# Causal mask of two grouped attentions: a DVE addition in the scores bank instead of two bf16 products per round

## The reference, cut to what matters

```python
# _L0_attn_b_ref: 32 query heads of 128, 8 key heads, rotary and compressed parts
scores = jnp.einsum('bhqd,bhkd->bhqk', q, k) * scale
causal = jnp.tril(jnp.ones((q_len, q_len), bool))
scores = jnp.where(causal[None, None], scores, jnp.asarray(-1000000000.0, dt))
attn = jax.nn.softmax(scores, axis=-1)
out = jnp.einsum('bhqk,bhkd->bhqd', attn, v)

# _L1_attn_a_ref: 32 heads, latent keys and values
scores = (jnp.einsum('bshd,bthd->bhst', q_nope, k_nope) + jnp.einsum('bshd,btd->bhst', q_pe, k_pe)) * scale
scores = jnp.where(causal[None, None], scores, jnp.finfo(scores.dtype).min)
probs = jax.nn.softmax(scores, axis=-1)
out = jnp.einsum('bhst,bthd->bshd', probs, v).reshape(b, s, NH * V_DIM)
```

## Time and profile before

| what | value |
|---|---|
| median of 3 runs | 2360.93 us |
| lowest and highest | 2348.55, 2364.01 us |
| the profiled execution: its own time | 2363.39 us |
| its span, first to last instruction | 2361.7 us |
| mean granted TensorE clock | 0.959 |
| attn0b's rounds, attn1a's rounds | about 540 to 1275 us, 1392 to 1887 us of the span |

### The profile page before, as it was taken

The page is one execution under the profiler, slowest core; times in us unless marked ns, Lnnn a source line. Parts: engine busy times, 40 slices in busy tenths (PEclk is TensorE's granted clock), DMA queues, the critical chain, the costliest instruction groups (busy, mean ns, idle before and its releaser), DMA issues. The chain is left out here.

```text
span 2361.7 us, 33423 instructions
## 1 busy us (share of the span) xinstructions
PE 2153.1 (91%) x11504; PEld 1480.1 (63%) x11504; DVE 1414.9 (60%) x2599; ACT 1093.5 (46%) x2639; POOL 840.2 (36%) x1062
## 2 busy tenths in 40 slices
PE   6999998887999999999997869999999986899988
PEld 4344366665777777777775656777777664554457
DVE  5777575416566556565663645666666555757756
ACT  4666653214444444444443535555555533325553
POOL 2000000534444444443442025555544412346621
PEclk9899999997999999999999979999999997989999
DMA  2000023651111111111110244433333201543310
GB/s 89 1 1 1 1 76 111 139 118 52 41 54 32 41 54 32 41 32 32 36 50 31 67 103 108 108 91 100 92 98 78 78 23 53 160 95 68 71 34 36
DMA packets 112542, 149.18 MB, mean 63 GB/s; under 512 B 39588, under 2 KB 52516, under 8 KB 110200
## 3 DMA queue, kind: packets, MB, share of 16 engines
q1 hardware_dynamic: 64376, 108.77, 16.3%
q0 software_dynamic: 48000, 38.28, 7.1%
HBM read 86.07 MB, written 27.26 MB: 48 GB/s over the span
## 5 line engine op out<-in xcount | busy, mean ns | idle before, releaser
L1842 POOL TENSOR_TENSOR attn0b_probs<-attn0b_probs,attn0b_recip 128x128 f32<-128x128 f32 (+3 forms) x256 | 192.5, 772 | 223.4 <-DVE attn0b_recip L2081 223.2
L2473 POOL TENSOR_TENSOR attn1a_probs<-attn1a_probs,attn1a_recip 128x128 f32<-128x128 f32 (+3 forms) x256 | 179.2, 721 | 232.9 <-DVE attn1a_recip L2656 232.3
L2529 ACT ACTIVATE attn1a_probs<-attn1a_scores,attn1a_negmax 128x128 f32<-128x128 f32 (+3 forms) x256 | 132.8, 524 | 174.5 <-DVE attn1a_negmax L2642 173.3
L1948 ACT ACTIVATE attn0b_probs<-attn0b_scores,attn0b_negmax 128x128 f32<-128x128 f32 (+3 forms) x256 | 132.8, 524 | 149.5 <-DVE attn0b_negmax L2074 148.3
L1956 ACT ACTIVATE attn0b_probsT<-attn0b_turned 128x128 f32<-128x128 f32 (+3 forms) x128 | 56.0, 438 | 245.7 <-PE attn0b_turned L2222 245.3
L2235 PE MATMUL attn0b_out<-attn0b_probsT,attn0b_v_now 128*128 128x512 f32 x320 | 155.6, 617 | 11.8 <-DVE attn0b_probsT L2088 11.8
L1468 DVE TENSOR_REDUCE attn0a_negmax<-attn0a_by_query 128x2 f32<-128x1024 f32 x128 | 152.3, 1219 | 21.3 <-PE attn0a_by_query L1555 21.3
L2642 DVE TENSOR_REDUCE attn1a_negmax<-attn1a_scores 128x2 f32<-128x256 f32 (+3 forms) x128 | 105.5, 824 | 70.6 <-PE attn1a_scores L2831 70.6
L2074 DVE TENSOR_REDUCE attn0b_negmax<-attn0b_scores 128x2 f32<-128x256 f32 (+3 forms) x128 | 104.8, 819 | 46.5 <-PE attn0b_scores L2211 46.5
L37 PE MATMUL attn0b_aux<-attn0b_wo_hi,attn0b_oT_hi 128*128 128x512 f32 x256 | 126.4, 494 | 1.4 <-DVE attn0b_oT_lo L2092 1.4
L2843 PE MATMUL attn1a_turned<-ident_f,attn1a_probs 128*128 128x128 f32 x640 | 115.8, 279 | 8.6 <-DVE attn1a_probsT L2650 7.2
(11 more groups left out here) (510 smaller groups left out, 6115.0 us busy)
## 6 DMA issues: line engine op xcount, KB each, us to landing
pre<-in_b_o SPq DMA_DIRECT2D x16, 1024.0 KB, 5.3
attn1a_qT<-attn1a_stage SPq DMA_DIRECT2D x128, 128.0 KB, 2.4
attn1a_qT<-attn1a_stage SPq DMA_DIRECT2D x64, 256.0 KB, 3.8
pre<-in_b_q SPq DMA_DIRECT2D x8, 1024.0 KB, 6.4
pre<-in_b_kv SPq DMA_DIRECT2D x5, 1024.0 KB, 5.8
attn0b_vals<-attn0b_v_out SPq DMA_DIRECT2D x16, 256.0 KB, 4.0
attn0b_keys_hi<-attn0b_part_hi POOLq DMA_DIRECT2D x32, 128.0 KB, 5.1
attn0b_keys_lo<-attn0b_part_lo POOLq DMA_DIRECT2D x32, 128.0 KB, 7.7
```

The lines of the kernel that those rows point to most:

```text
L1842: pool.tensor_tensor(x, x, recip[:, r % 2, e:e + 1].broadcast_to([P, (qt + 1) * P]), ALU.mult).then_inc(s_scaled, 1)
L1948: act.activation(probs[:, r % 2, e, 0:width], scores[r % 2][:, e, 0:width], ACT.Exp, bias=negmax[:, r % 2, e:e + 1], accum_out=sums[:, r % ...
L2473: pool.tensor_tensor(x, x, recip[:, r % DEEP, e:e + 1].broadcast_to([P, (qt + 1) * P]), ALU.mult).then_inc(s_scaled, 1)
L2529: act.activation(probs[:, r % DEEP, e, 0:width], scores[r % 2][:, e, 0:width], ACT.Exp, bias=negmax[:, r % 2, e:e + 1], accum_out=sums[:, ...
```

## The change

In both attentions the two bf16 products per round are gone, and the last product of the three is the one that ends the accumulation and signals the scores. DVE's `maximum` first adds the mask to the diagonal blocks of both heads, in place in PSUM, in one `tensor_tensor` of 2 x 128 elements per partition (bf16 mask, broadcast over the two heads), signals a new semaphore, waits for it, and then takes the maximum as before. Nothing else is moved.

```diff
--- before.py
+++ after.py
@@ -1722,6 +1722,7 @@
         s_c, s_e, s_rope, s_qadd, s_qhi, s_qlo, s_x = [n.sem(k) for k in ("c", "e", "rope", "qadd", "qhi", "qlo", "x")]
         s_scores, s_max, s_exp, s_recip, s_scaled, s_turned, s_pv, s_ohi, s_olo = [
             n.sem(k) for k in ("scores", "max", "exp", "recip", "scaled", "turned", "pv", "ohi", "olo")]
+        s_masked = n.sem("masked")
         s_copied = [n.sem("copied_first"), n.sem("copied_second")]
         s_raw = n.sem("raw")
         block = ctx.enter_context(nc.Block(no_gpsimd_drain=True))
@@ -2071,6 +2072,10 @@
             def maximum(r):
                 at, i, b, qt, p = place(r)
                 dve.wait_ge(s_scores, r + 1)
+                diagonal = scores[r % 2][:, :, qt * P:(qt + 1) * P]
+                dve.tensor_tensor(diagonal, diagonal, m.mask[:, 0:1, :].broadcast_to([P, PAIRS, P]),
+                                  ALU.add).then_inc(s_masked, 1)
+                dve.wait_ge(s_masked, r + 1)
                 dve.tensor_reduce(negmax[:, r % 2, :], scores[r % 2][:, :, 0:(qt + 1) * P], AX.X, ALU.max,
                                   negate=True).then_inc(s_max, 1)
 
@@ -2206,10 +2211,7 @@
                     into = scores[r % 2][:, e, 0:width]
                     pe.matmul(into, queries[0], keys[0], start=True, stop=False)
                     pe.matmul(into, queries[1], keys[0], start=False, stop=False)
-                    pe.matmul(into, queries[0], keys[1], start=False, stop=False)
-                for e in range(PAIRS):
-                    last = pe.matmul(scores[r % 2][:, e, qt * P:width], m.ident16[:, :], m.mask[:, 0, :],
-                                     start=False, stop=True)
+                    last = pe.matmul(into, queries[0], keys[1], start=False, stop=True)
                 last.then_inc(s_scores, 1)
 
             def turn(r):
```

## The result

| | median | runs |
|---|---|---|
| before | 2360.93 us | 5, from 2348.55 to 2367.4 |
| after | 2376.85 us | 5, from 2372.43 to 2381.78 |

The ratio is 1.0073, with a 95% interval of 1.0044 to 1.0102. The kernel became some 16 us slower. Forecast were 2350 us and a range up to 2371, so both the sign and the range were wrong. The profiled execution of the changed kernel took 2372.6 us, its span 2370.9.

A forecast was written before the change was run, and what follows sets the result against it. PE's queue was taken to set the pace of both attentions. Terms of -7.0 us (attn1a) and -5.4 (attn0b) made -12.4 from the profiled 2363.4, so 2351, put at 2350 us against the median; range 2330 to 2371.

The forecast's parts named there:

- DVE's addition: DVE between scores and maximum, each round: 0.425 us by element count plus the semaphore, 0.46 us more in all.
- Rival 2: DVE between scores and maximum: PSUM write costs 0.69 us, lengthening the softmax chain, 2370 us; with rival 3 chance 0.18.
- The ceiling: PE, both attentions: mask pairs cost 0.18 or 0.13 us, 19.8 us per attention, 39.7 us as most to gain.
- attn1a, -0.88 us a turn: attn1a: PE keeps 0.49 us of masks per 8-round period less 0.05, gaining 0.44, or 7 us over 16 periods.
- the round with qt 1: attn1a, second transposes after DVE's copy: 0.30 us spare, copy 0.33 later, PE 0.13 earlier, short by 0.16 once per period.
- The POOL wait: attn1a, every second qt 3 round: PE waits for POOL's scaling and starts +0.05 us from its old place.
- attn0b, -0.99 us a turn: attn0b, 8 tiles: -0.18 - 0.30 - 0.93 + 0.42 us a turn, -7.4 us over 7.5 turns.
- The late tile with qt 2: attn0b, qt 2 tile whose maximum is late behind DVE's output-weight split: the addition goes straight to PE, +0.42 us.
- The first rounds of both qt 1 tiles: attn0b: each gains 0.15 us from the first mask, with 0.03 us to the add that frees the projection bank.
- The last tiles of attn0b: attn0b, last 5 tiles, no projection left to cover the softmax: each 0.34 to 0.46 us longer, +2 us.
- rival 3: Both attentions, only a shuffle: savings and waits cancel within 5 us of 2363; with rival 2 chance 0.18.
- Theory E: From the experiments: without PE's products the clock is lower for longer in and behind changed stages; some 10 us given back.

The follow-up runs named there:

- experiment 5: Changed kernel, but DVE adds the mask only in rounds 2 and 4 of 16 in attn0b, 7 and 15 of 16 in attn1a: 2374.08 us in one run.

## Why the prediction was wrong

- **DVE's addition, 0.425 + 0.035 us.** Right: 0.427 and 0.430, and 0.03 to the maximum (1668.55 + 0.43 to 1669.02 shows 0.04). Rival 2, a dear write into PSUM, was not the cause. The Trainium skill (VectorE: DVE Perf Modes, The TRN2 errata) gives (N+151)/0.96 ns for an fp32 tensor-tensor operation. By that formula half an addition would take an estimated 291 ns; the rows have 298 in attn1a and 293 in attn0b.
- **The ceiling, 39.7 us.** Too high as a worth. A pair of products does cost 0.12 to 0.20 us of PE's queue in the distances that shorten without it, but in nine of 16 distances of attn0b and in four of 16 of attn1a PE spends this time waiting anyway, and the steady turns lose 1.17 and 1.70 us when nothing replaces the products. From first to last scores that is 6.1 us in attn0b and 11.9 in attn1a.
- **attn1a, -0.88 us a turn (0.44 a period).** It was +0.59. The step that failed is the round with qt 1: I had the copy's 0.30 us as spare, short by 0.16 against a PE that comes 0.13 earlier. PE doesn't come earlier there (ScalarE's copy holds it), and of the 0.30 only 0.15 can be used up. So the second transposes come 0.18 later and such a distance is +0.21, where the forecast came to 0.16 - 0.13 = +0.03. Nor did the other places swallow this, as "once per period" assumed. A loss behind the scores is added to each round that has it: four with qt 1 at +0.21 to +0.28, two with qt 0 at +0.07, and the rounds beside the absorbed and the output weights at +0.53 and +0.12, which I had at nothing. They sum to +1.76 against -1.16 of gains kept.
- **The POOL wait.** Foreseen and there: 14 waits, 0.21 us each. But it was to leave PE 0.05 us behind its old place, counted from the scores two rounds before the qt 3 round. PE is behind by 0.21 in one period and by 0.51 in the other (the transposes come 15.96 instead of 15.75 us behind those scores, and 17.98 instead of 17.47). It hangs little on PE's lead: with an addition in the qt 3 rounds alone and PE's products in all others (experiment 5), the distance still was +0.26.
- **attn0b, -0.99 us a turn.** It was -0.07. The late tile with qt 2 cost +0.43, as forecast (+0.42). Three other steps failed. The tile with qt 1 cost +0.32, since ScalarE's copy hangs on the exponentials and so on DVE, not on PE's projection alone. The first rounds of both qt 1 tiles gave 0 instead of -0.15, for the projection follows the add that frees its bank by 0.14 before and 0.15 after, again a smallest distance. And distance 7 was +0.16 instead of -0.13, for ScalarE's copy, held up by the addition of round 6. Together 0.32 + 0.30 + 0.29 = 0.91 us of the 0.92 missed.
- **The last tiles of attn0b, +2 us.** Measured +4.1 over rounds 112 to 126, but about 1.8 of it is clock. Distance 119 is +2.27 there and +0.45 in the version with both forms of the mask, and in the changed kernel a stretch of some 3.4 us at half clock falls into it, behind a window in which PE was busy 1.87 of 4 us:

```profile
1221.00:1225.00 4.00, 1.87 (x7) 0.90 (x6) 2.45 (x5) 2.35 (x6) 1.45 (x2) 1.00 0.00 0
1225.00:1229.00 4.00, 4.00 (x8) 1.85 (x7) 1.29 (x3) 1.45 (x4) 3.33 (x5) 0.57 0.52 154
```

The latency by itself is thus some 2.3 us, as forecast. Such stretches stand in the last turn in all seven profiles with additions there, in three of the eight with PE's products, and in the one without a mask.
- **The start and the end of attn1a.** Not in the forecast: +5.7 us in the first turn, with the clock at its half. The last step of the forecast named the clock as what would break the sum, but I had looked only at stretches in mid-stage. The last turn was taken for one like the others. It lost 2.5 us: where fewer projections cover the softmax, distances with qt 0 are +0.34 and those with qt 2 +0.59.
- **The rivals.** The outcome is rival 2's side with another mechanism: latency, but at the foreseen price of the addition. I tied it to a dearer instruction and so gave it, with rival 3, only 0.18, and 0.06 to more than 1% slower; it should have hung on how much of each end-to-start distance can be used.

In sum: attn0b +2.3 where -5.4 was forecast, attn1a +13.2 where -7.0 was. Of the former, 4.1 lie in the last turn, -0.5 in the seven others by latency and products, and -1.3 in less time at half clock, above all in the first turn; the version with attn0b alone, with before's first turn, shows +3.6. Of the latter, 5.7 lie in the first turn, 5 x 0.6 in the plain ones, 2.2 in the second (1.5 of it one short half-clock stretch), 2.5 in the last. Theory E as a whole stays open. Over its 56 runs beside the experiments the kernel before has a median of 103.7 us for span times (1 - mean clock), a measure of the time at half clock. The changed kernel has 114.0, attn0b alone 113.5, no mask 116.0, and the choices by round 103.3 and 100.7. Beyond the start of attn1a and the last turn of attn0b no profile shows where.

## What to carry to other kernels

The distance between a result's end and its use is spare only down to what the same pair of engines shows when it truly waits (here 0.15 us for a copy ahead of transposes, 0.10 ahead of the product with the values); subtract that first. Work taken from the busiest engine is worth only what it costs in rounds in which that engine isn't waiting, and latency put into a chain costs its full length in each round where the chain is tight, so price both round by round, and measure them apart: a version without the work and one with both. Where the answers differ by round, so can the code: the mask on DVE in the rounds that can bear it and on PE in the others beats the two kernels by 0.7% and 1.4% (the latter against runs of another session).

## What was not expected of the hardware

- Waits of 0.1 to 0.2 us often don't show as idle time, since the modelled end of a matmul (0.28 us for products 0.12 apart) covers them. A PE busy 99.84 of 100 us can be waiting in four distances of sixteen.
- The clock stayed at half for some 17 us in the first turn of attn1a in both profiles of the changed kernel and in that of the half addition. Within it stands a window in which PE was busy 3.88 of 4 us. In the same code with attn0b unchanged it was some 7 us (two windows of 4 us at 0.55 and 0.60).
- Two additions of sixteen carry all of what sixteen cost in a turn of attn0b when PE's products stay: +0.78 and +0.79 us.
